# Where x1 is transposed among the transposes at the head of each slot

## The reference

```
scores = q k^T / sqrt(48) + adj          (q, k, v from x, with biases)
ctx    = softmax(scores) v
x1     = rmsnorm(x + ctx wo + bo)
ff     = silu(x1 w1 + b1) w2 + b2
x2     = rmsnorm(x1 + ff)
out    = layernorm(x + x2)
```

## Time and profile before

| | |
|---|---|
| median of 3 runs | 2948.49 us (2948.18 to 2950.1) |
| the profiled execution's own time | 2949.07 us |
| its span, first to last instruction | 2947.3 us |
| TensorE busy: matmuls, weight loads | 2910.8 us (99%), 2857.1 us (97%) |
| VectorE, ScalarE, GpSimd busy | 1853.1, 1443.2, 684.8 us |
| mean granted TensorE clock | 0.997 |

### The profile page before, as it was taken

The page is one execution under the profiler, slowest core; times in us unless marked ns, Lnnn a source line. Parts: engine busy times, 40 slices in busy tenths (PEclk is TensorE's granted clock), DMA queues, the critical chain, the costliest instruction groups (busy, mean ns, idle before and its releaser), DMA issues.

```text
span 2947.3 us, 62438 instructions
## 1 busy us (share of the span) xinstructions
PE 2910.8 (99%) x25216; PEld 2857.1 (97%) x25216; DVE 1853.1 (63%) x3621; ACT 1443.2 (49%) x4258; POOL 684.8 (23%) x968
## 2 busy tenths in 40 slices
PE   7999999999999999999999999999999999999998
PEld 7999999999999999999999999999999999999998
DVE  6665656657666566566665665656656656566564
ACT  5544545545445455454454554544545445445442
POOL 0122222222222222222222222222221222222222
PEclk9999999999999999999999999999999999999999
DMA  5211212212112121121221211212212112122110
GB/s 164 80 51 53 69 40 64 57 52 64 48 56 69 40 64 56 54 64 44 60 64 46 64 53 52 68 42 62 61 48 64 53 51 69 41 63 60 49 46 28
DMA packets 155489, 171.91 MB, mean 58 GB/s; under 512 B 18624, under 2 KB 155200, under 8 KB 155200
## 3 DMA queue, kind: packets, MB, share of 16 engines
q1 hardware_dynamic: 151952, 166.92, 19.5%
q10 hardware_dynamic: 3248, 0.99, 0.2%
HBM read 92.35 MB, written 25.17 MB: 40 GB/s over the span
## 4 chain that ended last, share of the span: by engine, by line
PE 95%; ACT 3%; DVE 1%; DMA 1%; SPq 1%; issue 0%; POOL 0%; ACTq 0%; POOLq 0%
PE ps_work L448 47%; PE ps_rows L595 28%; PE ps_rows L448 7%; PE ps_att L526 4%; PE ps_att L477 4%; ACT probs L657 2%; PE ps_work L456 2%; PE ps_rows L510 1%; PE ps_rows L514 1%; PE ps_rows L456 1%; SPq L364 0%; DMA x_in<-in_x 0%; ACT probs L668 0%; DVE w_s L802 0%; DMA stage<-in_L_gnn_wq 0%
## 5 line engine op out<-in xcount | busy, mean ns | idle before, releaser
L448 PE MATMUL ps_work<-x1T,w_s 128*128 128x256 f32 x6912 | 823.2, 280 | 3.7 <-ACT h_raw L722 3.7
L448 PEld LDWEIGHTS ps_work<-x1T,w_s 128*128 128x128 f32 x6912 | 820.8, 188 | 3.9 <-ACT h_raw L722 3.9
L595 PE MATMUL ps_rows<-w_s,h 128*128 128x384 f32 x4608 | 824.0, 340 | 0.0
L595 PEld LDWEIGHTS ps_rows<-w_s,h 128*128 128x128 f32 x4608 | 810.6, 188 | 0.0
L722 ACT ACTIVATE h_raw<-ps_work,b_col 128x256 f32<-128x256 f32 x768 | 322.3, 471 | 534.8 <-PE ps_work L448 531.3
L668 ACT ACTIVATE probs<-probs,neg_max 128x128 f32<-128x128 f32 x1024 | 396.4, 390 | 158.2 <-DVE neg_max L827 158.2
L430 POOL TENSOR_TENSOR x<-x,rows 128x768 f32<-128x768 f32 x64 | 117.7, 1840 | 1165.4 <-DVE h L885 1165.4
L883 DVE CAST h<-h_raw 128x512 fp32r<-128x512 f32 x384 | 164.3, 428 | 313.8 <-ACT h_raw L722 313.8
L894 DVE TENSOR_TENSOR y<-ps_rows,x 128x384 f32<-128x384 f32 x128 | 71.4, 558 | 415.0 <-PE ps_rows L595 415.0
L885 DVE TENSOR_TENSOR h<-h_raw,h 128x512 fp32r<-128x512 f32 x384 | 265.9, 692 | 13.2
L697 ACT ACTIVATE squares<-y 128x384 f32<-128x384 f32 x128 | 66.6, 521 | 329.3 <-DVE y L894 329.3
(11 more groups left out here) (87 smaller groups left out, 3576.8 us busy)
## 6 DMA issues: line engine op xcount, KB each, us to landing
x_in<-in_x SPq DMA_DIRECT2D x128, 384.0 KB, 3.1
qk<-qk_flat SPq DMA_DIRECT2D x381, 96.0 KB, 2.3
x_last<-in_x SPq DMA_DIRECT2D x64, 384.0 KB, 3.6
out<-y SPq DMA_DIRECT2D x63, 384.0 KB, 2.7
bias<-in_adj SPq DMA_DIRECT2D x64, 128.0 KB, 2.1
qk<-qk_flat SPq DMA_DIRECT2D x127, 64.0 KB, 2.1
qk<-qk_flat SPq DMA_DIRECT2D x127, 32.0 KB, 2.0
stage<-in_L_gnn_w SPq DMA_DIRECT2D x17, 192.0 KB, 4.0
```

What stands on the lines that cost most here:

```text
L448: mm = pe.matmul(ps_out, stationary(sta), moving(mov), start=(i == 0), stop=(i == n - 1))
L595: mm = pe.matmul(ps_rows[b][:, 0:d], h[:, sta, m, b * P:(b + 1) * P], w2_s[:, mov, m, :], start=(m == 0 and i == 0), stop=(m == fc - 1 and ...
```

## The change

TensorE's order at the head of the slot becomes: `transpose_x`, `transpose_probs` of both graphs, `transpose_x1`, then both contexts and the scores. The third block of x1 goes into columns 512 to 767 of `ps_att[0]` in every slot, no longer into `ps_rows[1]`. Its transposes therefore wait for `probsT_ready[0]`, ScalarE's copy of the first graph's probabilities out of that tile. `context(g, 1)` no longer waits for `x1T_lo[1]`, but for `res2_ready[1]`, the reading of the feed-forward result out of `ps_rows[1]` in the slot before. `scores(g, 0)` gets a third wait, `x1T_lo[1]`. ScalarE copies both graphs' probabilities out before it turns to x1.

```
         def x1_third(g):
-            return ps_rows[1][:, 0:toks] if g < last else ps_att[0][:, 2 * toks:3 * toks]
+            return ps_att[0][:, 2 * toks:3 * toks]
...
                 for b in range(PAIR):
                     pe.wait_ge(x1_ready[b], through(g))
-                if g == last:
-                    pe.wait_ge(probsT_ready[0], through(g))
-                elif live(g - 1):
-                    pe.wait_ge(res2_ready[1], through(g - 1))
+                pe.wait_ge(probsT_ready[0], through(min(g + LAG_FF - LAG_ATTN, last)))
                 transpose_rows(x1_third(g), x1[:, g % 2], (2,), x1T_done[1])
...
-                elif live(g + LAG_ATTN - LAG_FF):
-                    pe.wait_ge(x1T_lo[1], through(g + LAG_ATTN - LAG_FF))
+                elif live(g + LAG_ATTN - LAG_FF - 1):
+                    pe.wait_ge(res2_ready[1], through(g + LAG_ATTN - LAG_FF - 1))
...
                 if live(g - 1):
                     pe.wait_ge(probsT_ready[b], through(g - 1))
+                if b == 0 and live(g + LAG_SCORES - LAG_FF):
+                    pe.wait_ge(x1T_lo[1], through(g + LAG_SCORES - LAG_FF))
...
                 if live(g_attn):
-                    transpose_probs(g_attn, 0)
+                    for b in range(PAIR):
+                        transpose_probs(g_attn, b)
                 if live(g_ff) and g_ff < last:
                     transpose_x1(g_ff)
                 if live(g_attn):
-                    transpose_probs(g_attn, 1)
                     for b in range(PAIR):
                         context(g_attn, b)
...
                 if live(g_attn):
-                    probsT_out(g_attn, 0)
+                    for b in range(PAIR):
+                        probsT_out(g_attn, b)
                 if live(g_ff) and g_ff < last:
                     transposed_hi(g_ff, 1, x1_third(g_ff), x1T_done, x1T, x1T_hi)
                 if live(g_attn):
-                    probsT_out(g_attn, 1)
                     context_hi(g_attn, 0)
```

## The result

The changed kernel takes 2962.57 us (median of 6 runs, 2960.44 to 2964.21), the kernel before 2948.65 us on the same occasion: a ratio of 1.0045 with a 95% interval of 1.0032 to 1.0058, which is 9.4 to 17.1 us; the medians are 13.9 us apart. The forecast was 2961.5 us, 13.0 slower. The profiled execution took 2963.41 us, with a span of 2961.6 and 1.8 around it.

What follows compares the result with a forecast made beforehand. TensorE, busy 99% of the span, bounds the kernel. Per slot a new wait costs 0.52 us and a removed one returns 0.31: net 0.21, times 62 slots 13.0 us, 2948.49 to 2961.5 us; range 2956.0 to 2966.5.

Steps and rivals of the forecast that it cites:

- The removed wait: TensorE before the second context: its wait for the probabilities' copy goes, gaining 0.30 to 0.31 us of a 0.37 gap.
- The new wait: TensorE before x1's third block: waits for ScalarE's copy out of the same tile, losing 0.51 to 0.52 us per slot.
- cheap start: Rival, 12%: x1's load starts 0.05 after the release instead of 0.11; +0.15 per slot, 9.3 us, 2957.8.
- Late keys: Rival, 12%: VectorE keeps its delay past the residual, so keys or scores come late; up to 3.7 us more, 2965.
- No change: Rival, 8%: the new wait costs about what it gives back, less than 0.2% (5.9 us); bounds give 2953.5.
- faster: Rival, 4%: copy L657 ends over 0.21 sooner relative to the transposes; 0.5 sooner would give 19 us, 2929.
- The sum: Net +0.21 us per slot over 62 slots: 13.0 us, median from 2948.49 to 2961.5, +0.44%.
- Slot 3: Its scores already wait for the DMA of q and k, so the loss is covered and the slot not counted.
- The scores cover it: Output product after the scores: needs both contexts' low parts, 0.52 later for context 0, but was forecast not to wait.
- The rule on banks: x1's block enters a bank under evacuation; taken alone the rule would mean 62 x 0.52 = 32 us more.

Runs made afterwards that it cites:

- The copy in halves: Changed kernel, but ScalarE copies ps_att[0] in two instructions, upper bank first with its own semaphore that x1 waits for: 2937.58 us, ratio 0.9957.
- the first blocks ahead: Changed kernel with x1's first two blocks (four transposes) ahead of its third: 2930.19 us, ratio 0.9936; run again 2931.27, ratio 0.9940.
- moving the wait: Changed kernel with transpose_x1 asking for probsT_ready[0] first of its three waits instead of last: 2958.55 us, ratio 1.0032.
- the last experiment: Changed kernel with two more VectorE instructions of 384 columns ahead of the keys in slots 5 to 63, result unused: 2975.85 us, ratio 1.0088.
- the tile alone: Changed kernel with TensorE's and ScalarE's order edits undone; x1's third block stays in ps_att[0] with the new waits: 3035.61 us, ratio 1.0290.
- both orders alone: Changed kernel's TensorE and ScalarE orders, but x1's third block in its old place ps_rows[1] with the old waits: 2962.09 us, ratio 1.0043.
- TensorE's order alone: TensorE's new order, x1's third block in ps_rows[1], ScalarE copying it between the two graphs' probabilities as before: 2937.59 us, ratio 0.9958.
- the kernel with both edits: Changed kernel with x1's first two blocks ahead of its third and the copy of ps_att[0] in halves, upper first: 2936.78 us, ratio 0.9960.

## Why the prediction was right

**The removed wait** was worth what the turns gave, 0.31 and not the gap's 0.37: from the first context to the scores it is now 1442.72 - 1440.84 = 1.88 us, forecast 1.89, before 2.20.

**The new wait** was the main term and right in size: forecast a start at 2.31 and a loss of 0.51 to 0.52, measured 2.32. The copy in halves and the first blocks ahead show that it is the unfinished copy and nothing else in the change: with 0.42 less of copy in front, or with four transposes over it, the sign turns. That the start after the release costs 0.11 and not 0.05 was argued from one row of slot 64; moving the wait showed it, at 4.0 to 4.5 us measured and 3.8 computed. The rival of the cheap start fell with the first trace, and is real under another order of the waits. (The Trainium skill, Perfetto Trace Analysis, Identifying Dependency Chains, on instructions put in front for additional waits: the runs agree, 0.12 and 0.11 with the late wait among the extra ones, 0.06 less with it first, and L484's instruction of 0.051 us is such a one.)

**Late keys** did not happen. VectorE's delay was 0.35 at the bias addition where 0.52 was forecast, and at the keys nothing more was left: 1454.51 - 1454.16 = 0.35 after the first values product, the same as 1447.88 - 1447.53 before:

```profile
1454.16 3.09 PEld L448 LDWEIGHTS ps_work<-wv_s,xT 128*128 128x128 f32 x18
...
1454.51 0.87 DVE L844 TENSOR_SCALAR qk_flat<-ps_work,bk_col 128x256 f32<-128x256 f32 x2
```

The mis-sizing changed nothing, and the slack, 0.28 net by the last experiment, was left whole.

**No change and faster** did not come, and both needed a shorter stall. The copy took 1.02 again. But the faster rival's mechanism is real: the halved copy is that case, at 0.60 instead of 1.02, and gave 2937.6.

**The sum.** Slot 3 was rightly left out: it lasts 50.92 us before and 50.94 after. 62 slots by 0.21 made 13.0; measured are 13.9 between the medians and 14.3 between the two profiled spans. The slot grew by 0.20 (45.43 to 45.63), so 62 of them make 12.4. A term was missed in slot 65, which has no scores: there the output product follows the contexts at once and waits for their low parts. Timeline of before, then of after:

```profile
2884.73 0.30 PEld L448 LDWEIGHTS ps_rows<-wo_s,ctxT 128*128 128x128 f32 x2 [0.29 <-DVE ctxT L814]
```

```profile
2899.03 1.01 PEld L448 LDWEIGHTS ps_rows<-wo_s,ctxT 128*128 128x128 f32 x6 [0.60 <-DVE ctxT L813]
```

The product starts 0.05 after VectorE's low part of the first graph's context, and that ends 2.23 after the first context's start in both kernels (2884.68 - 2882.45 and 2898.98 - 2896.75). The second context comes sooner, but TensorE then only waits longer for the low part of the first, so in this slot the 0.31 is not given back: 0.3 us once. "The scores cover it" holds in every slot but the one without scores. With it the slots make 12.7.

Of the 1.6 left in the difference of the spans, 0.6 was there at the start of slot 3 (62.19 before, 62.78 after), ahead of the first transposes of x1. The second profile of the changed kernel starts that slot at 60.38, so this is a difference between executions and none of the change. 1.0 arose behind slot 63; the last section shows where. That the medians came out 0.9 from the forecast is therefore in part luck: the interval alone is 4 us wide to either side.

**The rule on banks** (the Trainium skill, Perfetto Trace Analysis, Matmuls: rotate through different PSUM banks) pointed the right way, but 32 us would have been the price without the wait given back; measured are 14, so the sum from the rows was needed. With the banks as they are, other transposes put ahead took the stall away, which was worth 33 us.

## What to carry to other kernels

When small work is moved to where it waits for an evacuation, look at what else of it could stand in front: here two lines in another order, with everything else of the change kept, turned +0.45% into -0.6%. A gap that goes is worth the time by which the work behind it really moves up (0.31 here for a gap of 0.37), and a gap that comes costs the wait for the release plus the start behind it. Of several waits in front of one TensorE instruction, put the one that will be satisfied last first in the program; that was worth 0.06 us each time here. Test a tile and each engine's order one by one as well as together: the tile alone cost 86 us, both orders alone 13, all of it together 14, TensorE's order alone gained 12, and the tile with the right inner order gained 18 to 19.

## What was not expected of the hardware

The granted clock of TensorE falls once near the end of the program, inside slot 64's `up`, and for how long differs from run to run of one kernel. TensorE had stood idle there for 3.94 us (before) or 4.15 us (changed) until ScalarE's `h_raw` came. In the kernel before, the weight loads of `up` behind that wait, then busy time by stretch with the granted clock as the third figure from the end (0.50 is the level of 1.2 GHz):

```profile
2857.25 10.12 PEld L448 LDWEIGHTS ps_work<-x1T,w_s 128*128 128x128 f32 x72 [3.94 <-ACT h_raw L722]
...
2857.40:2860.80 3.40, 3.40 (x17) 3.40 (x18) 3.26 (x9) 0.53 (x2) 0.00 (x0) 0.50 0.60 174
```

The same in the first profile of the changed kernel:

```profile
2870.14 10.83 PEld L448 LDWEIGHTS ps_work<-x1T,w_s 128*128 128x128 f32 x72 [4.15 <-ACT h_raw L721]
...
2868.50:2875.30 6.80, 5.16 (x24) 5.16 (x25) 5.57 (x14) 3.15 (x7) 0.00 (x0) 0.50 0.37 116
```

And in its second profile:

```profile
2868.53 10.10 PEld L448 LDWEIGHTS ps_work<-x1T,w_s 128*128 128x128 f32 x72 [4.15 <-ACT h_raw L721]
...
2869.70:2873.10 3.40, 3.40 (x18) 3.40 (x17) 3.19 (x7) 0.84 (x2) 0.00 (x0) 0.50 0.73 231
```

In the first profile the clock fell while TensorE still stood idle and stayed low for 6.8 us, in the second it was low for 3.4 us, as in the kernel before. The 72 loads took 10.83 us against 10.10, and 10.12 before. Together with the wait, longer by 0.21 than before, this makes 0.9 of the 1.0 us that the first profile lost behind slot 63. Why the clock stayed low longer is not shown.

The two spans were 2961.6 and 2959.0. Of these 2.6 us all 2.6 were there at the start of slot 4 (113.73 and 111.13), the slots up to 63 took 0.02 each back (45.63 against 45.65), and 1.0 came behind it. So a difference of some 2 us between two single executions can come from the start and the end alone; the medians and the slots are the safer evidence.

The other surprise is the two paces of the large products, 9.46 and 9.57 us for the same 72 loads from the output product to the values products, at a granted clock of 1.00. A kernel can take either from one slot to the next, and the kernel with both edits took the slower one in nearly all of its slots. That cost it about 6 us (58 x 0.11), and the cause is open.
